# A graph kernel of four layers on one core: every state of the recurrent layer is turned by block transposition and DMA, and GpSimd takes over two kinds of elementwise work

## The reference

```
x = layernorm(x + L0(x, adj))     # (adj x + x) w + bias, rows divided by their length
x = layernorm(x + L1(x, adj))     # five gated steps, below
x = layernorm(x + L2(x, adj))     # one product with a normalized adjacency
x = layernorm(x + L3(x, adj))     # one product with softmax weights over the edges
def step(h):                      # L1, five times, av = [adj h, adj h]
    u3 = h @ u3_w.T + u3_b
    z = sigmoid(av @ w3_w.T + w3_b + u3)
    r = sigmoid(av @ w4_w.T + w4_b + u3)
    hv = tanh(av @ w5_w.T + w5_b + (r * h @ u5_w.T + u5_b))
    return (1 - z) * h + z * hv
```

## Time and profile before

| what | value |
|---|---|
| median of 3 runs | 741.76 us (741.48 to 742.01) |
| time of the profiled execution | 741.54 us, its span 739.6 us |
| PE busy | 732.2 us, 99% of the span |
| DVE busy | 641.3 us, 87% |
| ACT busy | 511.0 us, 69% |
| POOL busy | 160.6 us, 22% |
| DMA engines | queue of the kernel's transfers 20.5% of 16 engines |
| granted TensorE clock | 0.998 of full speed |

### The profile page before, as it was taken

The page is one execution under the profiler, slowest core; times in us unless marked ns, Lnnn a source line. Parts: engine busy times, 40 slices in busy tenths (PEclk is TensorE's granted clock), DMA queues, the critical chain, the costliest instruction groups (busy, mean ns, idle before and its releaser), DMA issues.

```text
span 739.6 us, 11592 instructions
## 1 busy us (share of the span) xinstructions
PE 732.2 (99%) x3612; PEld 607.3 (82%) x3612; DVE 641.3 (87%) x1505; ACT 511.0 (69%) x1057; POOL 160.6 (22%) x307
## 2 busy tenths in 40 slices
PE   9999999999999999999999999999999999999996
PEld 8888788888788888877777777778888888889886
...
DMA packets 106363, 39.22 MB, mean 53 GB/s; under 512 B 93888, under 2 KB 95424, under 8 KB 105664
## 3 DMA queue, kind: packets, MB, share of 16 engines
q1 hardware_dynamic: 106304, 38.50, 20.5%
...
## 4 chain that ended last, share of the span: by engine, by line
PE 91%; ACT 5%; DVE 2%; DMA 1%; issue 1%; SPq 0%; POOL 0%; POOLq 0%; ACTq 0%; DVEq 0%
PE agg_ps L1163 14%; PE agg_ps L1165 14%; PE agg_ps L1164 14%; PE gate_ps L1078 7%; PE gate_ps L1077 7%; PE gate_ps L1079 7%; PE cand_ps L1077 5%; PE cand_ps L1079 5%; PE cand_ps L1078 5%; PE gate_ps L1084 3%; PE cand_ps L1084 3%; PE turn_ps L1204 2%; ACT feat L581 1%; PE turn_ps L1208 1%; ACT res L488 1%; DMA rows<-in_adj 1%
## 5 line engine op out<-in xcount | busy, mean ns | idle before, releaser
L1163 PE MATMUL agg_ps<-adj_hi,nat_hi 128*128 128x512 f32 x384 | 155.3, 404 | 0.0
L1165 PE MATMUL agg_ps<-adj_hi,nat_lo 128*128 128x512 f32 x384 | 150.2, 391 | 0.0
L1164 PE MATMUL agg_ps<-adj_lo,nat_hi 128*128 128x512 f32 x384 | 149.8, 390 | 0.0
L696 POOL TENSOR_SCALAR shift<-mean_var 128x4 f32<-128x4 f32 x62 | 23.7, 383 | 412.0 <-DVE mean_var L939 410.1
L542 ACT ACTIVATE gate_r<-gate_ps,bias 128x512 f32<-128x512 f32 x80 | 55.2, 690 | 52.6 <-PE gate_ps L1079 52.6
L517 ACT ACTIVATE agg_hi<-agg_ps 128x512 fp32r<-128x512 f32 x80 | 48.2, 603 | 62.2 <-PE agg_ps L1165 62.2
L1165 PEld LDWEIGHTS agg_ps<-adj_hi,nat_lo 128*128 128x128 f32 x384 | 72.1, 188 | 15.8
L1164 PEld LDWEIGHTS agg_ps<-adj_lo,nat_hi 128*128 128x128 f32 x384 | 72.4, 188 | 13.6
L1163 PEld LDWEIGHTS agg_ps<-adj_hi,nat_hi 128*128 128x128 f32 x384 | 72.3, 188 | 13.2
L886 DVE TENSOR_TENSOR gate_r<-gate_r,feat 128x512 f32<-128x512 f32 x80 | 55.3, 692 | 30.6 <-ACT gate_r L542 30.5
L872 DVE TENSOR_TENSOR agg_lo<-agg_ps,agg_hi 128x512 fp32r<-128x512 f32 x80 | 55.0, 687 | 22.3 <-ACT agg_hi L517 22.1
...
## 6 DMA issues: line engine op xcount, KB each, us to landing
...
nat_lo<-state_blocks SPq DMA_DIRECT2D x168, 64.0 KB, 2.5
...
```

The costliest lines, as they stand in the source:

```text
L1163: pe.matmul(ps, nat_hi[:, b, k, :], m_hi[:, k, :], start=(k == 0), stop=False)
L1164: pe.matmul(ps, nat_hi[:, b, k, :], m_lo[:, k, :], start=False, stop=False)
L1165: last = pe.matmul(ps, nat_lo[:, b, k, :], m_hi[:, k, :], start=False, stop=(k == T - 1))
```

## The change

All 80 states of the steps now go by block transposition and DMA, the 22 others of the inner steps and the 16 results too, and PE turns none. The list BY_DMA, the lag STATE_LAG, the kinds "state" and "result" and the second DVE order go. POOL gets two operations on 128 x 512 tiles: the in-place low part of the 64 inner states (was on DVE), and the sum of residual and result, from nat_lo in SBUF, for the 16 last states (was on DVE, from PSUM). Both wait for agg_hi_made of the same slot, and stand at the head of POOL's slot. Feat_lo has one place in DVE's order, ahead of the new state. In the steps' norms stats moves from one slot after the add to two relative to the turn, norm and split one slot later as well, while turn_lag is changed so that most of them stay in the slot where they were. In the work for L2 and L3, the store of mix is cut into four parts issued three slots apart, SUM_AT is one slot later and L2_AT three, the store of row_d is issued by ACT, and the SP loop runs four slots further.

The diff, without lines that only declare semaphores or move constants:

```diff
 L0, L2, L3 = 0, STEPS + 1, STEPS + 2
 UNITS = B * (STEPS + 3)
 LAST = B * STEPS
-BY_DMA = [*range(17, 34, 2), 43, 45, *range(47, 78)]
 AFTER = B * (STEPS + 1)
-STATE_LAG = 4
-LAGS = {"turn": (0, 0, 0, 0), "add": (2, 1, None, None), "stats": (2, 1, 1, 1), "norm": (4, 3, 2, 2), "split": (5, 4, 12, None),
+LAGS = {"turn": (0, 0, 0, 0), "add": (2, 1, None, None), "stats": (2, 2, 1, 1), "norm": (4, 4, 2, 2), "split": (5, 5, 12, None),
         "cross": (5, None, 12, None), "back": (6, None, 13, None)}
 LAST_PROMPT = 10
...
 def turn_lag(u):
-    if is_inner(u):
-        return STATE_LAG
     if stage(u) == L0:
         return 2
     if not is_step(u):
         return 1
-    k = u - LAST
-    return STATE_LAG + k // 4 if k <= IN_STEP else k - 5
+    return max(5, u - LAST - 6)
 def lag(what, u):
...
-NORMED = sorted((u for u in range(UNITS) if not is_inner(u)), key=lambda u: (u + turn_lag(u), -u))
+NORMED = sorted((u for u in range(UNITS) if not is_inner(u)), key=lambda u: (u + turn_lag(u) + lag("stats", u), -u))
...
 CHOSEN_AT = [B + 10 + 3 * k for k in range(T)]
 LATE_AT = [at + 2 for at in CHOSEN_AT]
 VALUE_AT = [at + 2 for at in CHOSEN_AT]
-SUM_AT = VALUE_AT[-1] + 2
+SUM_AT = VALUE_AT[-1] + 3
 WHOLE_AT = SUM_AT + 2
-L2_AT = WHOLE_AT + T
+L2_AT = WHOLE_AT + T + 2
 assert L2_AT + T <= 4 * B
 DIAG_AT = LAST
...
     found = []
-    if is_inner(s - STATE_LAG) and s - STATE_LAG not in BY_DMA:
-        found.append(("state", s - STATE_LAG))
...
     if s in VALUE_AT:
         found.append(("value", VALUE_AT.index(s)))
-    found += [("result", u) for u in norms_at(s, "turn") if is_step(u)]
...
 SWAP_LAG = 5
 Z_BEHIND = 0
-TURNED = [u for u in range(B, LAST) if u not in BY_DMA]
 def swaps(u):
-    return sum(v <= u and v % 2 == u % 2 for v in BY_DMA)
-def dense(s):
-    return s - SWAP_LAG - 1 in BY_DMA
+    return (u - B) // 2 + 1
 def read_by_act(turn):
...
             def slot(s):
                 u = s - 3
-                if u in BY_DMA:
-                    sp.wait_ge(swapped, nth(BY_DMA, u))
+                if is_step(u):
+                    sp.wait_ge(swapped, u - B + 1)
                     sp.dma_start(swap_dram[u % B], cand[:, u % 2, :]).then_inc(swap_out[u % 2], 16)
                 u = s - 4
-                if u in BY_DMA:
+                if is_step(u):
                     sp.wait_ge(swap_out[u % 2], 16 * swaps(u))
                     if swaps(u) > 1:
                         sp.wait_ge(swap_in[u % 2], 16 * BLOCKS * (swaps(u) - 1))
...
+                if s - 1 in VALUE_AT:
+                    k = VALUE_AT.index(s - 1)
+                    sp.wait_ge(max_made, k + 1)
+                    sp.dma_start(mix_dram.rearrange("(p t) m -> p t m", t=T)[:, k, :], mix[:, k, :]).then_inc(mix_stored, 16)
...
-                    sp.wait_ge(max_made, T)
-                    sp.dma_start(mix_dram.rearrange("(p t) m -> p t m", t=T), mix[:, :, :]).then_inc(mix_stored, 16)
...
-            for s in range(AFTER):
+            for s in range(AFTER + 4):
...
                 u = s - 2
                 if is_step(u):
                     act.wait_ge(cand_done, u - B + 1)
-                    if u - 2 in BY_DMA:
+                    if u >= B + 2:
                         act.wait_ge(swap_out[u % 2], 16 * swaps(u - 2))
-                    elif u >= B + 2:
-                        act.wait_ge(state_made, u - B - 1)
                     act.activation(cand[:, u % 2, :], cand_ps[u % 2][:, :], ACT.Tanh,
                                    bias=bias[:, B_H:B_H + 1]).then_inc(cand_made, 1)
                 u = s - 1
...
                     if u > B:
                         act.wait_ge(cand_done, u - B)
                     act.activation(reset_hi[:, :], gate_r[:, u % 2, :], ACT.Copy).then_inc(reset_hi_made, 1)
-                u = s - STATE_LAG
-                if is_inner(u) and u not in BY_DMA:
-                    k = TURN_NO["state", u]
-                    act.wait_ge(turned, k + 1)
-                    act.wait_ge(agg_done, u + 1)
-                    act.activation(nat_hi[:, u % B, :, :], turn_ps[k % 2][:, :].rearrange("p (t d) -> p t d", t=T),
-                                   ACT.Copy).then_inc(state_hi_made, 1)
                 u = s - SWAP_LAG
-                if u in BY_DMA:
+                if is_inner(u):
                     act.wait_ge(swap_in[u % 2], 16 * BLOCKS * swaps(u))
                     act.activation(flat(nat_hi[:, u % B, :, :]), flat(nat_lo[:, u % B, :, :]).bitcast(F32),
                                    ACT.Copy).then_inc(swap_hi_made, 1)
...
+                if s == SUM_AT + 3:
+                    act.wait_ge(row_d_made, 1)
+                    act.dma_start(d_dram[0].rearrange("(t p) -> p t", p=P), row_d[:, :],
+                                 allow_slow_non_contiguous=True).then_inc(d_stored, 16)
...
             def slot(s):
+                u = s - SWAP_LAG - 1
+                if is_inner(u):
+                    pool.wait_ge(swap_hi_made, u - B + 1)
+                    pool.wait_ge(agg_hi_made, s + 1)
+                    pool.tensor_tensor(flat(nat_lo[:, u % B, :, :]), flat(nat_lo[:, u % B, :, :]).bitcast(F32),
+                                       flat(nat_hi[:, u % B, :, :]).bitcast(F32), ALU.subtract).then_inc(swap_lo_made, 1)
+                for n in norms_at(s, "add"):
+                    if is_step(n):
+                        pool.wait_ge(swap_in[n % 2], 16 * BLOCKS * swaps(n))
+                        pool.wait_ge(agg_hi_made, s + 1)
+                        pool.tensor_tensor(res[:, n % B, :, :], nat_lo[:, n % B, :, :].bitcast(F32), res[:, n % B, :, :],
+                                           ALU.add).then_inc(result_made, 1)
                 if s == 2:
                     pool.wait_ge(param_in, PARAMS)
...
                                 out=res[:, b, t, :], in0=layer_ps[n % 4][:, t * D:(t + 1) * D],
                                 scalar=length[:, n % 4, t:t + 1], in1=res[:, b, t, :], op0=ALU.mult, op1=ALU.add)
                         last.then_inc(rows_read, 1)
-                    else:
-                        dve.tensor_tensor(res[:, b, :, :], turn_of("result", n)[:, :].rearrange("p (t d) -> p t d", t=T),
-                                          res[:, b, :, :], ALU.add).then_inc(turn_read, 1)
                 if AFTER <= s < UNITS:
                     wait_normed(dve, s - B)
...
                     dve.wait_ge(z_made, u - B + 1)
                     dve.tensor_tensor(cand[:, u % 2, :], cand[:, u % 2, :], gate_z[:, u % 2, :],
                                       ALU.mult).then_inc(move_made, 1)
-                u = s - SWAP_LAG - 1
-                if u in BY_DMA:
-                    dve.wait_ge(swap_hi_made, nth(BY_DMA, u))
-                    dve.tensor_tensor(flat(nat_lo[:, u % B, :, :]), flat(nat_lo[:, u % B, :, :]).bitcast(F32),
-                                      flat(nat_hi[:, u % B, :, :]).bitcast(F32), ALU.subtract).then_inc(swap_lo_made, 1)
-                if is_step(s) and not dense(s):
+                if is_step(s):
                     dve.wait_ge(feat_hi_made, s - B + 1)
                     dve.tensor_tensor(feat_lo[:, :], feat[:, s % B, :], feat_hi[:, :].bitcast(F32),
                                       ALU.subtract).then_inc(feat_lo_made, 1)
...
                     dve.wait_ge(reset_hi_made, u - B + 1)
                     dve.tensor_tensor(reset_lo[:, :], gate_r[:, u % 2, :], reset_hi[:, :].bitcast(F32),
                                       ALU.subtract).then_inc(reset_lo_made, 1)
-                if is_step(s) and dense(s):
-                    dve.wait_ge(feat_hi_made, s - B + 1)
-                    dve.tensor_tensor(feat_lo[:, :], feat[:, s % B, :], feat_hi[:, :].bitcast(F32),
-                                      ALU.subtract).then_inc(feat_lo_made, 1)
-                u = s - STATE_LAG
-                if is_inner(u) and u not in BY_DMA:
-                    dve.wait_ge(state_hi_made, nth(TURNED, u))
-                    dve.tensor_tensor(nat_lo[:, u % B, :, :],
-                                      turn_ps[TURN_NO["state", u] % 2][:, :].rearrange("p (t d) -> p t d", t=T),
-                                      nat_hi[:, u % B, :, :].bitcast(F32), ALU.subtract).then_inc(turn_read, 1)
                 for n in norms_at(s, "stats"):
                     i = NORMED.index(n)
                     if n == UNITS - 1:
                         last_norm(i)
                         continue
                     if is_step(n):
-                        dve.wait_ge(turn_read, reads(TURN_NO["result", n]))
+                        dve.wait_ge(result_made, nth([v for v in NORMED if is_step(v)], n))
                     elif n < B:
                         dve.wait_ge(rows_read, nth(ADDED, n))
                     else:
...
                     if s < B:
                         pe.wait_ge(x_lo_made, s + 1)
                     elif 2 * B <= s < AFTER:
-                        if s - B in BY_DMA:
```

(10 more changed lines are left out.)

18 lines of the change are left out of this document (8 added, 10 removed).

## The result

The changed kernel takes **751.21 us** (median of 4 runs, 750.75 to 752.26) against 741.76: ratio 1.0128, 95% interval 1.0116 to 1.0141. It is slower, by 1.3%, which the interval sets clear of no change, and the prediction of 737.5 us was wrong.

| stretch | before | forecast | after | after less forecast |
|---|---|---|---|---|
| start and tail (before sum 0, behind sum 111) | 98.57 | 98.6 | 99.10 | +0.5 |
| sums 0 to 20 | 87.45 | 87.45 | 87.44 | 0 |
| 20 to 88 | 438.06 | 430.5 | 433.30 | +2.8 |
| 88 to 97 | 58.82 | 63.8 | 66.82 | +3.0 |
| 97 to 111 | 56.70 | 55.0 | 62.74 | +7.7 |

A forecast was written before the change was run, and what follows sets the result against it. PE was taken as the bound over long stretches, DVE in slots 88 to 96. 741.54 - 10.7 (turns gone) + 6.4 (collisions) = 737.2 us, median 737.5; forecast 734 to 740.3, range 730 to 746.

The forecast's parts named there:

- PE's work in slots 20 to 87: Slots 20 to 87: without PE's turns the stretch falls from 438.06 to 430.2 us, a gain of 7.9 us.
- POOL's operation: POOL's new 128 x 512 operation: estimated 1.3 us; low parts of inner states covered up to 1.7 us, costing 0.
- Those of slots 23 and 25: Two early norms of L0 put POOL's low part late in slots 23 and 25: 0.3 us in all.
- the rival of long low parts: POOL's low parts outlast their cover; at 2.0 us, 19 us more over 62 slots, about 756 us; chance 0.13.
- The result adds: Last step: POOL's adds collide with DVE's two-input SBUF operations, 0.76 us each at full price; all collisions sum to 6.4 us.
- the second rival: POOL-DVE collisions cost the whole reading, 1.08 us each, 10.6 us in all: 741.7 us, 740 to 744; chance 0.22.
- its sign, slots of 7.6 us: Slots 90 to 95: slots of 7.6 us would show that collisions cost the whole reading.
- the first rival: Collisions cost next to nothing, as POOL waits and DVE does not: 731.1 us, 729 to 734; chance 0.20.
- The base without collisions: Slots 88 to 96, DVE the limit: 58.2 us before collision costs, a gain of 0.6 us.
- five turns give back 2.2 us where PE is the bound: Slots 97 to 105: five turns taken off PE at 0.44 us each gain 2.2 us.
- the adds there: Slots 99 to 105: four POOL adds meet a DVE that loses its own add: 0.5 us.
- DMA: 38 more round trips taken as 0; the 1 MB load in slot 38 may delay one state 0 to 2.5 us once.

The follow-up runs named there:

- light transfers: Changed kernel with the second 1 MB load cut to 256 KB, the diagonal's load and inverse roots' store in 16-byte pieces: 747.02 us, ratio 1.0067.
- Low part early: Changed kernel with POOL's low part one slot sooner, behind ACT's high part, without the wait for agg_hi: 813.46 us, one run.
- small add: Changed kernel with POOL's add of result and residual cut to 4 of 512 columns, its place and waits kept: 736.84 us, ratio 0.9937.
- No add: Changed kernel with POOL's adds of the results and their waits taken out, statistics waiting for the transfer: 737.22 us, ratio 0.9943.
- fills: Changed kernel with POOL's add replaced by three fills of the same width, same place and waits, reading no SBUF: 739.44 us, ratio 0.9966.
- The seven kernels with these transfers: The change and the follow-up kernels with the same transfers in slots 40 and 44 to 47, which take 34.5 to 36.2 us together.

## Why the prediction was wrong, step by step

**PE's work in slots 20 to 87: right.** Forecast 430.2 us; 433.30 less the 3.1 of the late transfers is 430.2, and light transfers took 429.03. Steady slots took 6.27, and the wait at reset_lo came 58 times in this stretch.

**POOL's operation: right.** 1.3 us estimated, 1.30 measured alone. Of the 64 low parts 61 were covered, as argued. Those of slots 23 and 25, which the prediction had set apart, met the product (1.78 us), and that of slot 46, behind the late transfers, a small DVE operation for L2 (1.27 us instead of 0.29). Low part early shows what the cover is worth, and the rival of long low parts is out.

**The result adds: the step that failed first, a term mis-sized.** I took 0.76 us for a collision, four times the delay seen at 128 columns, and ranked the whole reading behind it. It was 1.10 (1.78 less 0.69 in slot 93): the second rival's mechanism at its price, and its sign, slots of 7.6 us, came. DVE lost it, so the first rival is out. This is also what the Trainium skill says (SBUF — State Buffer, "Who interferes with whom"): each excludes the other for the whole instruction. A row of a quarter of the size had been no ground to go below it. I also gave 0.5 to slots 88 and 89, where DVE had a little time free, and let 96 and 97 go free. Measured, the slots from sum 89 to 97 took 7.36 to 7.71 us each with the add and 6.25 to 6.58 with the small one: eight full prices, 8.8 us, where 5.6 were forecast. The add of slot 96 was not free either: from sum 97 to 98 it is 5.16 us against 4.23 with the small add, 0.9 us that the table counts in the third stretch. The base without collisions, 58.2, was right (57.96 to 58.04).

**Sums 97 to 111: two steps failed, 7.7 us.** First, "five turns give back 2.2 us where PE is the bound": PE was it only while it had turns to do. No add leaves 56.90, not 54.5 (+2.4). Second, the adds there: 0.5 us forecast, 5.8 measured, in three parts: 0.6 for the add's place and wait (small add less no add), 2.45 for POOL's queue (fills less small add), 2.8 for reading (after less fills), of which 0.9 is the add of slot 96. I had asked who is blocked on DVE, and not what stands behind the add on POOL: the factor and shift of the next norm, for which ACT waits, for whose result DVE's seed waits, for which PE waits. That the last part is the lock alone is not strictly shown, since the add is up to 0.4 us longer than the fills.

**DMA: 0 taken, 3.1 us paid.** The bound of 2.5 us for the 1 MB load in slot 38 held (slot 40: 7.52 us, 6.46 with it light). The second place, slots 44 to 47 (26.94 us, 24.94 with light transfers), I had not seen: a store of 2 KB. The seven kernels with these transfers paid 3.1 to 4.8 us in the two places, measured against light transfers, and the change the least. The prediction counted bytes and round trips, and the harm came from 512 pieces.

**The sum.** 2.8 + 3.0 + 7.7 + 0.5 at the start and tail (scatter: they take 98.4 to 99.4 us in the other runs) is the whole distance from 737.2 to the 751.18 us of the profiled execution. Whole collisions everywhere were in the rivals (741.7); what put the time beyond the range, 730 to 746, is the stretch from sum 97 to 111, in layer L2: without its 7.7 us it would have been 743.5. There PE was taken for the bound, and each add was priced as if POOL's queue had no one behind it.
